# One-pass products of two parts for self attention's query, key and value blocks, and the layer norms' deviation multiplied in behind the products

## What is computed

```python
def _layernorm(x, axis=-1, eps=1e-05):
    m = jnp.mean(x, axis=axis, keepdims=True)
    v = jnp.var(x, axis=axis, keepdims=True)
    return (x - m) / jnp.sqrt(v + eps)

x = x + xattn(_layernorm(x), ctx_2048, ...)
x = x + attn(_layernorm(x), ...)
x = x + ffn(_layernorm(x), ...)

# self attention: 16 heads of 128
q = _mxfp4_matmul(x, wq_codes, wq_scales) + bq      # 512 -> 2048; k and v likewise
scores = jnp.einsum('bqhd,bkhd->bhqk', q, k) / jnp.sqrt(jnp.float32(HEAD_DIM))
attn = jax.nn.softmax(scores, axis=-1)
out = jnp.einsum('bhqk,bkhd->bqhd', attn, v).reshape(B, S, NUM_HEADS * HEAD_DIM)
return _mxfp4_matmul(out, wo_codes, wo_scales) + bo

# experts: gate, then a gated product
logits = x @ gate_w.T; scores = sigmoid(logits)     # top 4 of 32 in the top 2 of 4 groups
h = silu(x @ w1) * (x @ w3); y = (h @ w2) * weight_of_the_expert
```

## Time and profile before

| | |
|---|---|
| median of 3 runs | 1222.29 us (1221.86 to 1223.95) |
| the profiled execution | 1220.66 us, span 1218.9 us |
| PE busy | 1177.8 us (97%) |
| DVE, ACT, POOL busy | 951.7 (78%), 829.1 (68%), 763.6 (63%) us |
| the chain that ended last | PE 90%, POOL 4%, DVE 3% |
| PE L1554 in the chain | 4% of the span |

### The profile page before, as it was taken

The page is one execution under the profiler, slowest core; times in us unless marked ns, Lnnn a source line. Parts: engine busy times, 40 slices in busy tenths (PEclk is TensorE's granted clock), DMA queues, the critical chain, the costliest instruction groups (busy, mean ns, idle before and its releaser), DMA issues.

```text
span 1218.9 us, 26290 instructions
## 1 busy us (share of the span) xinstructions
PE 1177.8 (97%) x8746; PEld 929.7 (76%) x8746; DVE 951.7 (78%) x1643; ACT 829.1 (68%) x1833; POOL 763.6 (63%) x1063
## 2 busy tenths in 40 slices
PE   6999999999999999999999999999998779899998
PEld 4767888888888878888888888888886535588886
DVE  4668888888888878888788888888887723399997
ACT  5567777777777777777777777777777703377775
POOL 7988888888888878788888888887872000000000
PEclk9999999999999999999999999999999999999999
DMA  7146587566676666866657766668653998469990
GB/s 258 34 100 160 154 214 179 165 178 170 177 206 167 166 167 163 216 164 179 170 158 197 198 163 167 177 164 216 165 141 88 309 390 337 156 243 358 363 364 26
DMA packets 132400, 236.74 MB, mean 194 GB/s; under 512 B 18086, under 2 KB 45222, under 8 KB 131884
## 3 DMA queue, kind: packets, MB, share of 16 engines
q1 hardware_dynamic: 132268, 235.06, 65.6%
HBM read 140.87 MB, written 17.04 MB: 130 GB/s over the span
## 4 chain that ended last, share of the span: by engine, by line
PE 90%; POOL 4%; DVE 3%; issue 1%; ACT 1%; DMA 1%; SPq 0%; POOLq 0%; DVEq 0%; ACTq 0%
PE ps L1447 36%; PE ps L1310 18%; PE ps L1473 9%; PE ps L1517 8%; PE ps L1554 4%; PE ps L1634 3%; PE ps L1637 3%; PE ps L1640 3%; PE ps L1655 1%; PE ps L1663 1%; PE ps L1659 1%; PE ps L1611 1%; POOL cx_blocks L603 1%; POOL cx_blocks L605 1%; DVE small L1126 1%
## 5 line engine op out<-in xcount | busy, mean ns | idle before, releaser
L1447 PE MATMUL ps<-w_text,cx_blocks 128*128 128x512 f32 x1974 | 536.6, 397 | 1.3 <-ACT v_first L791 0.7
L1447 PEld LDWEIGHTS ps<-w_text,cx_blocks 128*128 128x128 f32 x1974 | 366.4, 189 | 65.8 <-issue 2.5
L834 ACT ACTIVATE p<-ps,small 128x512 f32<-128x512 f32 (+2 forms) x400 | 271.6, 679 | 202.3 <-DVE small L1128 199.3
L1126 DVE TENSOR_REDUCE small<-ps 128x1 f32<-128x512 f32 (+2 forms) x400 | 270.6, 677 | 110.5 <-PE ps L1473 110.1
L1310 PE MATMUL ps<-ident,p 128*128 128x128 f32 x1584 | 239.3, 273 | 8.8 <-DVE pt L1119 6.9
L1310 PEld LDWEIGHTS ps<-ident,p 128*128 128x128 f32 x1584 | 193.6, 140 | 63.8 <-issue 12.7
L1473 PE MATMUL ps<-k_stack,q_stack 96*128 96x512 f32 (+1 forms) x400 | 191.9, 480 | 0.8 <-ACT p L834 0.8
L816 ACT ACTIVATE pt<-ps 128x512 f32<-128x512 f32 (+1 forms) x250 | 147.7, 591 | 12.5 <-PE ps L1310 8.4
L605 POOL TENSOR_TENSOR cx_blocks<-cx_sum,cx_blocks 128x256 fp32r<-128x256 f32 x188 | 139.3, 741 | 14.7
L603 POOL TENSOR_TENSOR cx_blocks<-cx_sum,small 128x256 fp32r<-128x256 f32 x188 | 118.6, 631 | 44.5 <-PE ps L1447 36.7
L1128 DVE TENSOR_TENSOR small<-small 128x1 f32<-128x1 f32 x400 | 132.4, 331 | 13.7
(11 more groups left out here) (239 smaller groups left out, 1935.4 us busy)
## 6 DMA issues: line engine op xcount, KB each, us to landing
expert<-experts SPq DMA_DIRECT2D x34, 1536.0 KB, 8.7
k_stack<-kt_hi SPq DMA_DIRECT2D x384, 128.0 KB, 2.4
cx<-ctx_t SPq DMA_DIRECT2D x48, 512.0 KB, 4.2
k_stack<-kt_lo SPq DMA_DIRECT2D x192, 128.0 KB, 2.5
codes<-codes SPq DMA_DIRECT2D x64, 256.0 KB, 4.3
code_scale<-code_scales SPq DMA_DIRECT2D x256, 64.0 KB, 3.8
scaled<-codes SPq DMA_DIRECT2D x64, 256.0 KB, 4.3
weight_q<-scaled SPq DMA_DIRECT2D x1, 4096.0 KB, 14.2
```

Of the source, the lines that this page charges most:

```text
L834: eng.activation(pb[:, lo:hi], score_bank(s, h)[:, lo:hi], exp, bias=nm[1 - par][:, h:h + 1], accum_out=ls[1 - par][:, h:h + 1]).then_inc( ...
L1126: eng.tensor_reduce(ngm[:, h:h + 1], score_bank(s, h)[:, lo:hi], AX.X, ALU.max, negate=True).then_inc(e_gm, 1)
L1447: last = eng.matmul(ps_a[(p + i + 1) % 2][:, :], blk[:, i, a, c * P:(c + 1) * P], w_t[:, i, w, c * D:(c + 1) * D], start=(i in FRESH and c ...
```

## The change

**Products.** For q, k and v, ACT copies each block's weights (128 x 4 x 512) as fp32r to one of three buffers `weight_hi` (`self_high`), DVE subtracts the copy from the whole, in place (`weight_lo`, `self_low`). The transposed input becomes `ynt_hi` (ACT's copy) and `ynt_lo` (DVE's subtraction). `project` makes three groups of four products: high by high, high input by low weights, low input by high weights. The third buffer of `weight_hi` lies where `wo` is, so block 2's copy waits for the output projection of cross attention; each later one waits for the block three before it.

**Norms.** `center` takes the place of `layernorm` for the second and third norm: it subtracts the mean and doesn't wait for POOL. The deviation comes in later: as the scalar of the bias addition, as the scale of Silu and (negated by POOL, `rstd_neg`) of the router's exponential, in the gate weights (one more multiplication on DVE), and as the factor of the shared expert's hidden product.

**Order.** The transposes of k blocks 0 and 1 come ahead of v block 0, those of 2 and 3 behind it.

```diff
+        weight_lo = {n: sb(f"weight_lo_{n}", off * KB, [P, NWT, D], F32R) for n, off in (("q", 0), ("k", 32), ("v", 64))}
+        NWH = 3
+        weight_hi = [sb(f"weight_hi{i}", at * KB, [P, DC, D], F32R) for i, at in enumerate((184, 128, 144))]
...
+            eng.wait_ge(e_rs, 4)
+            eng.tensor_scalar(rstd_neg, rstd, -1.0, None, ALU.mult).then_inc(e_rs, 1)
...
+            def self_high(i):
+                if i % NB == 0:
+                    eng.wait_ge(e_wl[QKV[i // NB]], 16)
+                if i == NWH - 1:
+                    eng.wait_ge(e_ap, 1)
+                elif i >= NWH:
+                    eng.wait_ge(e_pj, i + 1 - NWH)
+                eng.activation(weight_hi[i % NWH][:, :, :], self_block(weight, i), copy).then_inc(e_shi, 1)
+
+            self_high(0)
             eng.wait_ge(e_at, 1)
...
+            self_high(1)
+            self_high(2)
             eng.wait_ge(e_lnt, 1)
-            eng.activation(ynt[:, :], ps_t[:, :], copy).then_inc(e_lntc, 1)
+            eng.activation(ynt_hi[:, :], ps_t[:, :], copy).then_inc(e_lntc, 1)
...
+            for i in range(NWH, 2 * NB - 1):
+                self_high(i)
+            for b in range(NB):
+                if b < NB - 1:
+                    self_high(2 * NB - 1 + b)
+                store_heads(0, b)
+            self_high(3 * NB - 2)
+            for b in range(NB):
+                store_heads(1, b)
+            self_high(3 * NB - 1)
...
+            eng.wait_ge(e_rs, 5)
+            eng.activation(score, ps_lg[:, 0:NE], exp, scale=rstd_neg).then_inc(e_lge, 1)
...
-                eng.activation(m_a[n % 2][:, :], ps_h[n % 2][:, 0:NF], ACT.Silu).then_inc(e_act, 1)
+                eng.activation(m_a[n % 2][:, :], ps_h[n % 2][:, 0:NF], ACT.Silu, scale=rstd).then_inc(e_act, 1)
...
-            def layernorm(dst, src, done=None):
+            def center(dst, src):
                 chain(eng.bn_stats(stats, src))
                 eng.bn_aggr(mv, stats).then_inc(e_var, 1)
-                eng.wait_ge(e_rs, next(n_rsqrt))
-                last = eng.tensor_scalar(dst, src, mv[:, 0:1], rstd, ALU.subtract, ALU.mult)
+                eng.wait_ge(e_var, next(n_centered))
+                eng.tensor_scalar(dst, src, mv[:, 0:1], None, ALU.subtract).then_inc(e_ln, 1)
...
+            self_low(0)
+            self_low(1)
             eng.wait_ge(e_xb, 1)
             eng.wait_ge(e_ap, 1)
             eng.tensor_tensor(x1[:, :], ps_a[0][:, :], x_again[:, :], ALU.add).then_inc(e_x1, 1)
...
-                eng.tensor_tensor(part, ps_pj[b % 2][:, :], part, ALU.add).then_inc(e_pjb, 1)
+                eng.wait_ge(e_rs, 3)
+                eng.scalar_tensor_tensor(part, ps_pj[b % 2][:, :], rstd, part, ALU.mult, ALU.add).then_inc(e_pjb, 1)
...
+            chain(eng.tensor_tensor(wrec, wrec, rstd, ALU.mult))
...
-                for c in range(DC):
-                    last = eng.matmul(ps_pj[b % 2][:, :], ynt[:, c * P:(c + 1) * P], weight[n][:, c * NB + b, :],
-                                      start=(c == 0), stop=(c == DC - 1))
+                eng.wait_ge(e_shi, i + 1)
+                for c in range(DC):
+                    eng.matmul(ps_pj[b % 2][:, :], ynt_hi[:, c * P:(c + 1) * P], high[:, c, :], start=(c == 0), stop=False)
+                eng.wait_ge(e_slo, i + 1)
+                for c in range(DC):
+                    eng.matmul(ps_pj[b % 2][:, :], ynt_hi[:, c * P:(c + 1) * P], low[:, c, :], start=False, stop=False)
+                if i == 0:
+                    eng.wait_ge(e_ylo, 1)
+                for c in range(DC):
+                    last = eng.matmul(ps_pj[b % 2][:, :], ynt_lo[:, c * P:(c + 1) * P], high[:, c, :], start=False, stop=(c == DC - 1))
```

More of the change, by code:

```diff
@@ L116, in program @@
         zero_col, ln_eps, rms_eps, minus_half = (small[:, i:i + 1] for i in range(208, 212))
-        one_col = small[:, 221:222]
+        one_col, rstd_neg = small[:, 221:222], small[:, 222:223]
         k_t, r_t = small[:, 212:212 + GT], small[:, 220:221]
@@ L146, in program @@
         x1 = sb("x1", 194 * KB, [P, D])
-        yn, ynt = sb("yn", 198 * KB, [P, D]), sb("ynt", 200 * KB, [P, D])
+        yn = sb("yn", 198 * KB, [P, D])
+        ynt_hi, ynt_lo = (sb(f"ynt_{n}", at * KB, [P, D], F32R) for n, at in (("hi", 200), ("lo", 202)))
         s_max, s_nb, s_sum, s_rec = (small[:, i:i + SH] for i in (0, 16, 32, 48))
@@ L312, in mask, with self_block @@
             return 0, GK
+        def self_block(array, i):
+            return array[QKV[i // NB]][:, :, :].rearrange("p (c b) f -> p b c f", b=NB)[:, i % NB]
         N_POOL = 2 + 2 + 2 + 1 + 1 + 2 + 4
@@ L897, in _, with store_heads @@
             eng.activation(xnt[:, TA:], ps_s[0][:, 0:P], copy).then_inc(e_atc, 1)
+            self_high(1)
+            self_high(2)
             eng.wait_ge(e_lnt, 1)
-            eng.activation(ynt[:, :], ps_t[:, :], copy).then_inc(e_lntc, 1)
[L902 to L905, removed]
+            eng.activation(ynt_hi[:, :], ps_t[:, :], copy).then_inc(e_lntc, 1)
+            def store_heads(i, b):
+                eng.wait_ge(e_tr, NB * i + b + 1)
+                eng.activation((sqt, skt)[i][:, b * 512:(b + 1) * 512], ps_tr[b % 2][:, :], copy).then_inc(e_trc, 1)
+            for i in range(NWH, 2 * NB - 1):
[8 more added lines that the diff above has]
+            self_high(3 * NB - 1)
             for b in range(NB):
@@ L962, in chain @@
                 eng.wait_ge(e_dve, n_dve[0])
-            n_rsqrt = iter((3, 4))
-            def layernorm(dst, src, done=None):
+            n_centered = iter((2, 3))
+            def center(dst, src):
                 chain(eng.bn_stats(stats, src))
                 eng.bn_aggr(mv, stats).then_inc(e_var, 1)
-                eng.wait_ge(e_rs, next(n_rsqrt))
-                last = eng.tensor_scalar(dst, src, mv[:, 0:1], rstd, ALU.subtract, ALU.mult)
-                return chain(last) if done is None else last.then_inc(done, 1)
+                eng.wait_ge(e_var, next(n_centered))
+                eng.tensor_scalar(dst, src, mv[:, 0:1], None, ALU.subtract).then_inc(e_ln, 1)
             def split_weight(i):
@@ L1190, in _, with self_low @@
             steps(eng, step)
+            def self_low(i):
+                eng.wait_ge(e_shi, i + 1)
+                eng.tensor_tensor(self_block(weight_lo, i), self_block(weight, i), weight_hi[i % NWH][:, :, :].bitcast(F32),
+                                  ALU.subtract).then_inc(e_slo, 1)
+            self_low(0)
+            self_low(1)
             eng.wait_ge(e_xb, 1)
@@ L1204, in add_bias @@
                 eng.wait_ge(e_pj, NB * QKV.index(n) + b + 1)
-                eng.tensor_tensor(part, ps_pj[b % 2][:, :], part, ALU.add).then_inc(e_pjb, 1)
-            for n in "qk":
-                for b in range(NB):
-                    add_bias(n, b)
+                eng.wait_ge(e_rs, 3)
+                eng.scalar_tensor_tensor(part, ps_pj[b % 2][:, :], rstd, part, ALU.mult, ALU.add).then_inc(e_pjb, 1)
+            eng.wait_ge(e_lntc, 1)
+            eng.tensor_tensor(ynt_lo[:, :], ps_t[:, :], ynt_hi[:, :].bitcast(F32), ALU.subtract).then_inc(e_ylo, 1)
+            self_low(2)
+            for i in range(2 * NB):
+                add_bias(QKV[i // NB], i % NB)
+                self_low(i + NWH)
             eng.wait_ge(e_bo, 16)
@@ L1285, in _ @@
             for n in range(NX):
-                g = one_col if n < NSH else gw[:, n - NSH:n - NSH + 1]
+                g = rstd if n < NSH else gw[:, n - NSH:n - NSH + 1]
                 eng.wait_ge(e_act, n + 1)
@@ L1591, in _ @@
                 transpose_heads("q", b)
-            for b in range(NB - 1):
-                transpose_heads("k", b)
+            transpose_heads("k", 0)
+            transpose_heads("k", 1)
             project("v", 0)
-            transpose_heads("k", NB - 1)
+            transpose_heads("k", 2)
+            transpose_heads("k", 3)
             for b in range(NB):
```

11 lines of the change are left out of this document (6 added, 5 removed).

## The result

The changed kernel takes 1212.23 us (median; 1208.08 to 1212.53) where the kernel before took 1223.12 on the same chip: a ratio of 0.9907, 95% interval 0.9889 to 0.9925. The forecast was 1212.8, with a range of its own from 1211.0 to 1214.5. The profiled execution took 1212.08 us (span 1210.0) against 1220.66 (span 1218.9). The forecast is 0.6 us off; the gain that it added up, 9.5, is 1.4 short of the 10.9 between the medians.

What follows compares the result with a forecast made beforehand. TensorE was taken as the bound, with twelve self attention blocks in a row. 8.3 + 0.55 + 0.9 - 0.15 - 0.1 = 9.5 us gained, from the median of 1222.29 to 1212.8 us; range 1211.0 to 1214.5.

Steps and rivals of the forecast that it cites:

- Blocks on PE: Self attention's q, k and v blocks: twelve one-pass products take 2.75 us instead of 3.44, 8.3 us gained over twelve blocks.
- ACT and DVE feed it: Splits in q and k blocks: DVE's round is 2.88 us, but its head start keeps PE from waiting; margin 1 to 2.
- The rival: DVE's splits in self attention: from about 3.7 us a subtraction on, slower than before; 2%.
- Waits on ACT's queue: Head copies between ACT's splits: PE's second k transposes wait about 0.5 us instead of 0.34, 0.15 lost.
- Bias row: Output bias load in self attention: lands at 1013.8, DVE reaches it at about 1017.5, no wait, 3.7 us to spare.
- First norm: Norm ahead of self attention: 0.88 us gained by not waiting for POOL, 0.3 lost, net 0.55 gained.
- The hold: First norm, on DVE: the residual's addition stands behind block 1's subtraction, 0.3 us lost.
- Second norm: Norm behind self attention: 1.12 us from aggregation to subtraction shrinks to 0.23, 0.9 gained.
- Experts, nothing: Expert loop: Silu's pointer scale adds at most some 0.1 us, hidden in ACT's 0.93 idle; no change.
- Clock as left: Behind both later norms: half-clock stretches of 3.6 and 7 us stay, costing 1.8 and 3.5, unchanged in the sum.
- the rival given 20%: At the norms: shorter PE idle stretches keep the clock up, winning 1.8, 3.5 or 5.3 us more; 20%.
- The second price: Behind the second norm: the 7 us at half clock cost 3.5 us, won if the clock doesn't fall there.

Runs made afterwards that it cites:

- e6: The changed kernel without the products with self attention's low weight part and without DVE's subtractions that make it; 1203.34 us, ratio 0.9849.
- e4: The changed kernel with one idle DVE copy of the low part onto itself behind every subtraction; 1223.07 us, ratio 1.0012.
- e1: The kernel before with only the products of two parts and their splits, norms as before; 1213.29 us, ratio 0.9916.
- e7: The kernel before, with Silu reading its scale per partition from a column of ones; 1223.65 us, ratio 1.0015.
- e2: The kernel before with only the norms' deviation moved behind the products, blocks still four f32 products; 1217.94 us, ratio 0.9959.
- e8: The changed kernel with nine idle products in PE's queue at each of the two later norms; 1207.84 us, ratio 0.9885.
- e5: The changed kernel with two idle DVE copies of the low part onto itself behind every subtraction; 1239.55 us, ratio 1.0152.

## Why the prediction was right

- **Blocks on PE, 8.3.** Measured 8.34 with all waits, 0.91 us for four products as taken; q 2.72 (2.75 predicted), k 1003.27 to 1006.48 = 3.21 (3.19). One product costs 0.227 us at full clock, and e6 shows the same slope. The Trainium skill ("TensorE: Matmul & The Clock Gate", Back-to-back issue gap) has about 131 ns for each; the estimate from it was 1.57 for a block, and the measurement decides against it here.
- **ACT and DVE feed it.** Subtraction 2.28, round 2.86 (2.88). PE waits for no low part. e4 shows how little is to spare: 1.26 us more a round and all is lost, the fall of the clock there included. The rival put break-even at a subtraction of about 3.7 from start to start, and e4 stands at 2.20 + 1.26 = 3.46 with a result of zero: its mechanism is shown, and its point was a little too high.
- **Waits on ACT's queue.** Predicted 0.5 ahead of the second k transposes, measured 0.34 as before; the lost 0.15 didn't come. The wait for the normed probabilities is 0.38, 0.04 more than before, where 0.1 was allowed. Bias row: reached at 1017.81 (1017.5 predicted), no wait; e6 shows the wait once that margin is used up.
- **First norm, 0.55.** 0.98 gained at the hand-over (0.88). The hold, 0.3 in the sum, is in e1 with 0.28 but not in this trace, where the slow projection covers it. Predicted start of the first block 986.8, measured 987.53: the clock of the projection, 1.45, which nothing in the change's sum stands for.
- **Second norm, 0.9.** 0.96.
- **Experts, nothing.** 0.23 lost, 0.19 of it once, between the first two m_h (4.52 instead of 4.33); e7 and e2, with Silu's pointer, have 4.55 and 4.51, e1 without it 4.45. About 0.1 is the longer Silu ahead of ACT's copy of the next weights, for whose low part PE now waits; the rest stays open. The steady loop is unchanged at 4.33. The prediction's bound on the pointer's price, some 0.1 us, doesn't follow from its two rows (a quarter of the 1.92 us copy would leave 0.23); it came out at 0.089 all the same.
- **Clock as left.** Right in the profiled execution for both norms, and the sum of the steps, 9.5, is the 9.6 at equal clock. PE's idle stretches were 2.35 and 2.25 us (2.7 and 2.3 in the prediction), and the clock fell behind both, so the rival given 20% didn't come in this trace. The medians differ by 10.9, 1.3 more than at equal clock; whether that is mean clock or the scatter of four runs on each side isn't shown. The second price, 3.5 us for the low level behind the second norm, was too high: e8 got 2.29 for it, because the router's chain on DVE stood next. The step that took "the clock" for one fact of the kernel, read from one trace, was too simple: it differs from run to run, in places that the change doesn't touch.

The other misses are tenths: 0.29 more in the blocks (two waits that weren't longer), 0.43 more at the first norm (the hold covered, the hand-over 0.1 better), 0.06 more at the second, 0.2 lost behind it. They make the 10.1 us of this trace out of 9.5. That the median came out within 0.6 us of the forecast is partly luck: the gain was larger by 1.4, and the kernel before slower by 0.8 in the same series.

## What to carry over

Cost a bound engine's step by rows of the same instruction elsewhere in the trace, and then count the round of each feeding engine, with the order in its queue: here the gain was PE's to the tenth, and one more 1.2 us operation on DVE would have cancelled it. Look up in advance which transfer or addition stands next in line (here the bias row, 4 us behind), because the next improvement ends there. Compare stages between landmarks, not only medians, when the clock moves a run by 3 us, and look whether a slow stretch is in other traces too before it is put down to the change.

## What was not expected of the hardware

- One program's runs spread by 7 us (41 runs of before), along with a mean granted clock of 0.987 to 0.993. The level falls to half for about 3.5 or about 7 us after stretches in which PE had little to do, and not at the same places in each run: the projection of cross attention took 3.67 us in three traces and 4.93 or more in eleven, on the same instructions.
- Eighteen idle products, which fit into the waits of the two norms, kept PEclk at 1.00 there and won 4.0 us in the two stages behind the norms (ratio 0.9885 against 0.9907 and 0.9916 without them); they cost 0.05 us from aggregation to transposes at most (0.81 against 0.76).
- Waits make waits dearer: with 1.9 to 2.4 us of idle PE ahead of four blocks and 5.77 ahead of the probabilities (e5) 8 stretches ran at half clock instead of 5, and 7 of the 17 us lost against before were the clock's (by the fit).
- An fp32r copy of 128x2048 onto itself took 1.23 us on DVE, the subtraction of the same size 2.29.
